# Second picks of the aggregation weighed by VectorE in one instruction a part, and the closing bias laid by two wide products

## The chip, the core and the metric

The kernel runs on one core of one Trainium2 chip. The core has TensorE (PE, matrix products into PSUM), VectorE (DVE), ScalarE (ACT), GpSimd (POOL, here mostly the issuer of indirect and adding DMAs) and SyncE (SP, an issuer of plain DMAs); 16 DMA engines move the data. The metric is the device time of one execution in microseconds, as the median of several runs.

## The reference, cut to what matters

```python
h = relu(layernorm(x))                                   # 6250 nodes x 128
hid  = relu(h[src] @ W1[:128] + h[dst] @ W1[128:] + b1)  # one row per edge, 200000 edges
mask = sigmoid(hid @ W2 + b2)
w    = mask / (segment_sum(mask, src)[src] + 1e-9)
agg  = segment_sum(w[:, None] * h[dst], src)             # <- the aggregation
emb  = where(deg > 0, 0.5 * h + 0.5 * agg, h)
x    = x + relu(emb @ Wl + bl)                           # <- the closing product and its bias
# then layernorm, four graph convolutions by segment_max, and the sum with x
```

## The kernel before, in words

The program has stages one after the other; names of tiles begin with the letter of the stage. Stage a computes the masks of the edges, stage b (from 1720 to 2602 us) aggregates, stage c runs the four convolutions and takes nearly the whole second half. The change lies in stage b alone.

The 6250 nodes are 49 tiles of 128 (TILES = 49), and the targets are seven ranges of seven tiles (RANGES = RANGE = 7; RCOLS = 896 columns). Stage b builds, for each range `cb` and each source tile `u`, a block: a matrix `mass` of 128 source nodes by 896 target nodes that holds mask values. There are 343 blocks, numbered k = 49*cb + u. They go through a ring of 16 buffers (M_RING). One block is made in these steps:

- **heat(k)**, VectorE, L2004: one comparison writes six parts of 128 columns as zeros and ones into `onehot` (three buffers; it waits until ACT has used block k-3, `weighed_made`).
- **ACT, L1924**: six multiplications of one part each, by a mask per partition, into `mass[k % 16]`; it waits first for `hot` and for a free buffer (`wait_free`).
- **weigh_rest(k)**, VectorE, L2013: the seventh part in one instruction, after its own `wait_free`.
- **second picks**: a block whose u is a multiple of seven (TWICE, 49 of the 343) gets a second set. `heat_twice(k)`, VectorE, L2022, compares seven parts into `onehot_2`; ACT weighs them in seven multiplications into `extra` (L1933); `add_extra(k)`, VectorE, L2031, adds `extra` to `mass` in one operation of 896 columns. It stands two blocks later in VectorE's order (EXTRA_LAG = 2), behind `heat(k+2)` and `weigh_rest(k+2)`.
- **POOL, L1894**: when the block is weighed (and, for a block of TWICE, `extra_added`), an adding DMA of 448 KB brings the slow edges' masks from memory on top of the buffer. POOL issues them in the order of k, so a block that is not ready holds all later ones.
- **PE, L1983**: two products of the landed block with `h_row` (512 and 384 columns) add up `agg`; after every fourth block, and after u = 48, `total_bands` (L1956, L1959) adds up the columns into `totals`, and only its last products set `multiplied`, which frees the buffers: the ring is freed in groups of four (`free_by`).

The end of a range is spread over the next one. At u = 8 ACT copies the band sums (`copy_sums`, L1915), for which it must wait until PE has finished all 49 blocks of the range before. At u = 3 PE forms the totals (`total_up`, L1946). At u = 21 VectorE runs `embed` (L2041 to L2052, seven operations, one of them a reciprocal), and during it makes no comparison. PE waits for its result at u = 14 (`multiply`, `emb_made`), since PE stands some blocks behind VectorE. `multiply` forms emb @ Wl + bl: seven products of 128 columns with `wl` (L1968), and behind each a product of one row, ones by `bl` (L1970), that adds the bias. At u = 34 VectorE runs `join` (L2057 and on). For the last range all this follows with nothing beside it, and stage c starts behind it.

In this text block 21 means the block with u = 21 of its range, and 0 is the start of ACT's copy of the band sums in the third range (cb = 2), at 1969.90 us of the trace.

Of the kernel before, what the change touches and what calls it, by code (L numbers as in the profile page):

```python
# [16 lines left out]
P = 128  # L17
NODES = 6250
EDGES = 200000
D = 128  # L20
TILES = -(-NODES // P)
# [27 lines left out]
HEAD, TAIL = 4, 3  # L49
# [79 lines left out]
def bc(ap, shape):  # L129
    return ap.to_broadcast(shape)  # L130


def gnn(nc, x_in, src_in, dst_in, w1_in, b1_in, w2_in, b2_in, wl_in, bl_in,
# [20 lines left out]
    with ExitStack() as whole:  # L154
# [1622 lines left out]
        with ExitStack() as ctx:  # L1777
# [7 lines left out]
            onehot_2 = sb("b_onehot_2", [P, RANGE, P], BF16)  # L1785
            extra = sb("b_extra", [P, RANGE, P])
            ones_first = sb("b_ones_first", [P, P])
# [8 lines left out]
            wl = sb("b_wl", [P, D])  # L1796
            bl = sb("b_bl", [1, D])
            stats = sb("b_stats", [P, RANGE, 6])
# [12 lines left out]
            hot_2 = sem("b_hot_2")  # L1811
            extra_made = sem("b_extra_made")
            extra_added = sem("b_extra_added")
# [28 lines left out]
            def _(sp):  # L1842
                sp.dma_start(wl[:, :], wl_in).then_inc(w_loaded, 16)
                sp.dma_start(bl[:, :], bl_in.rearrange("(o n) -> o n", o=1)).then_inc(w_loaded, 16)

# [58 lines left out]
            def _(act):  # L1904
# [12 lines left out]
                for k in range(BLOCKS):  # L1917
                    cb, u, e = k // TILES, k % TILES, k % 3
                    if cb and u == SUMS_AT:
                        copy_sums(cb - 1)  # L1920
                    act.wait_ge(hot, k + 1)
                    wait_free(act, k)
                    for c in range(SCALED):
                        last = act.mul(mass[k % M_RING][:, c, :], onehot[e][:, c, :],  # L1924
                                       mask_r[:, u, cb * RANGE + c:cb * RANGE + c + 1])
                    last.then_inc(weighed_made, 1)
                    if k in TWICE:
                        i = TWICE.index(k)
                        act.wait_ge(hot_2, i + 1)
                        if i:  # L1930
                            act.wait_ge(extra_added, i)
                        for c in range(RANGE):
                            last = act.mul(extra[:, c, :], onehot_2[:, c, :],  # L1933
                                           mask_2[:, u // RANGE, cb * RANGE + c:cb * RANGE + c + 1])
                        last.then_inc(extra_made, 1)
                    if cb and u == JOIN_AT:
                        finish(cb - 1)
# [4 lines left out]
            def _(pe):  # L1942
# [22 lines left out]
                def multiply(cb):  # L1965
                    pe.wait_ge(emb_made, cb + 1)
                    for c in range(RANGE):
                        pe.matmul(product[cb % 2][:, c, :], emb_t[:, c * P:(c + 1) * P], wl[:, :], start=True,  # L1968
                                  stop=False)
                        last = pe.matmul(product[cb % 2][:, c, :], ones[0:1, :], bl[0:1, :], start=False, stop=True)  # L1970
                    last.then_inc(product_made, 1)
# [24 lines left out]
            def _(dve):  # L1996
# [20 lines left out]
                def heat_twice(k):  # L2017
                    cb, u, i = k // TILES, k % TILES, TWICE.index(k)
                    full, first = [P, RANGE, P], cb * RANGE
                    if i:  # L2020
                        dve.wait_ge(extra_made, i)
                    dve.tensor_tensor(onehot_2[:, :, :],  # L2022
# [3 lines left out]
                def add_extra(k):  # L2026
                    i = TWICE.index(k)
                    dve.wait_ge(weighed_made, k + 1)
                    dve.wait_ge(rest_weighed, k + 1)
                    dve.wait_ge(extra_made, i + 1)  # L2030
                    dve.tensor_tensor(mass[k % M_RING][:, :, :], mass[k % M_RING][:, :, :], extra[:, :, :], ALU.add  # L2031
                                      ).then_inc(extra_added, 1)

# [633 lines left out]
```

## Time and profile before

| what | us |
|---|---|
| median of 3 runs | 4972.48 (4972.26 to 4973.69) |
| the profiled execution | 4971.88 |
| its span in the trace | 4970.1 |
| stage b in it | 1720 to 2602 |
| the copies of the band sums | 1849.8, 1969.9, 2090.6, 2209.7, 2330.7, 2450.0, 2569.2 |

From one copy of the band sums to the next is one period of 49 blocks: 120.1, 120.7, 119.1, 121.0, 119.3 and 119.2 us. In the views below a row of a timeline gives the start in us, the length in us, the engine, the line and what is written from what, with the count of merged instructions and, in brackets, the idle time ahead and what ended it. A table by windows gives for each stretch the busy us of each engine and the number of its instructions, then the granted clock of TensorE (1.00 is 2.4 GHz, 0.50 is 1.2 GHz), the mean busy share of the 16 DMA engines and the GB/s. That share can be a little over one, since packets overlap.

### The profile page before, as it was taken

Reading aid. Unit: us, or ns where it says so; the run is one execution under the profiler, and the core shown is the slowest. Engines: PE = TensorE matmul, PEld = TensorE weight load, DVE = VectorE, ACT = ScalarE, POOL = GpSimd, SP = SyncE. Lnnn points to the kernel's source line nnn. Section 1 sums busy time; section 2 is a strip of 40 time slices with the busy share of each in tenths; the row PEclk is TensorE's granted clock in tenths of the full one; section 3 lists DMA queues with packets and bytes.
Section 4 is the critical chain, followed back from the end, with each engine's and each line's share of the span. In section 5 each row is a group of like instructions: output and inputs, shape, how many; then the busy total and the mean of one; then the engine's idle time right before and its main releaser. Section 6 shows DMA issues by size and latency. Waiting matters only on the chain. (4 is left out here: it accounts for less than half of the span.)

```text
span 4970.1 us, 48372 instructions
## 1 busy us (share of the span) xinstructions
PE 3739.1 (75%) x16011; PEld 1589.9 (32%) x16011; DVE 3885.0 (78%) x5124; ACT 943.7 (19%) x2780; POOL 3103.7 (62%) x3043
## 2 busy tenths in 40 slices
PE   1801068766766399999976989798987898969897
PEld 0401022222222134444432434333433343424343
DVE  4698488877877567777757888798887988878887
ACT  0100010000000198888841000010001000010000
POOL 5200377777777534444435777777776777767777
PEclk9999579988888799999988999899998999989998
DMA  9995365544545399999965444444444444444443
GB/s 361 397 402 233 87 201 168 169 144 145 172 139 154 98 211 206 208 208 209 207 138 157 135 140 136 118 141 132 140 130 126 137 133 133 132 134 135 140 137 95
DMA packets 359755, 843.42 MB, mean 170 GB/s; under 512 B 97017, under 2 KB 174559, under 8 KB 359327
## 3 DMA queue, kind: packets, MB, share of 16 engines
q0 software_dynamic: 137488, 313.46, 29.3%
q1 hardware_dynamic: 172624, 436.91, 24.9%
q10 hardware_dynamic: 49392, 89.94, 5.7%
q8 instruction: 128, 2.10, 0.2%
q14 instruction: 123, 1.01, 0.1%
HBM read 597.79 MB, written 242.28 MB: 169 GB/s over the span
## 5 line engine op out<-in xcount | busy, mean ns | idle before, releaser
L2429 PE MATMUL c_wide<-c_choice,c_parts 128*128 128x512 fp8e4 x8232 | 1881.7, 387 | 283.1 <-DVE c_odd L2514 136.9
L2303 POOL DMA_INDIRECT c_ring<-table,near x1288 | 1293.6, 1004 | 445.7 <-issue 327.9
L2429 PEld LDWEIGHTS c_wide<-c_choice,c_parts 128*128 128x128 bf16 x8232 | 797.8, 99 | 1337.2 <-DVE c_odd L2514 195.8
L2514 DVE TENSOR_TENSOR c_odd<-c_odd,c_wide 128x1024 f32<-128x1024 f32 x644 | 783.5, 1217 | 55.5 <-PE c_wide L2429 52.7
L2514 DVE TENSOR_TENSOR c_even<-c_even,c_wide 128x1024 f32<-128x1024 f32 x672 | 817.5, 1217 | 8.1 <-PE c_wide L2429 1.9
L1529 PE MATMUL a_wide<-a_choice,a_parts 128*128 128x512 fp8e4 x2058 | 526.6, 402 | 181.9 <-DVE a_hidden L1612 168.8
L1924 ACT ACTIVATE b_mass<-b_onehot,mask_r 128x128 f32<-128x128 bf16 x2058 | 607.2, 387 | 100.2 <-DVE b_onehot L2004 73.9
L1983 PE MATMUL b_agg<-b_mass,b_h_row 128*128 128x512 f32 (+1 forms) x1372 | 561.0, 558 | 74.1 <-DMA b_mass<-masks 74.0
L1894 POOL DMA_DIRECT2D b_mass<-masks x343 | 299.6, 962 | 475.5 <-ACT b_mass L1924 359.7
L1612 DVE TENSOR_TENSOR a_hidden<-a_wide,a_minus_bt 128x1024 f32<-128x1024 f32 x343 | 417.1, 1216 | 132.4 <-PE a_wide L1529 132.1
L1414 POOL DMA_INDIRECT masks<-a_value,a_cell x379 | 428.1, 1130 | 115.5 <-issue 114.6
L1406 POOL DMA_INDIRECT a_ring<-table_a,near x322 | 343.0, 1065 | 103.1 <-issue 92.6
L2004 DVE TENSOR_TENSOR b_onehot<-pick_of,up_row 128x768 bf16<-128x768 bf16 x343 | 327.7, 955 | 71.2 <-ACT b_mass L1924 69.3
L1983 PEld LDWEIGHTS b_agg<-b_mass,b_h_row 128*128 128x128 f32 x1372 | 254.0, 193 | 375.8 <-issue 290.7
L2368 ACT ACTIVATE c_h_t<-c_product,c_b 128x512 f32<-128x512 f32 (+1 forms) x56 | 35.5, 634 | 1775.3 <-PE c_product L2459 1775.3
L2543 DVE TENSOR_TENSOR c_ring<-c_ring 128x256 f32<-128x256 f32 (+5 forms) x444 | 219.2, 494 | 194.5 <-DMA c_ring<-table,near 167.9
L1529 PEld LDWEIGHTS a_wide<-a_choice,a_parts 128*128 128x128 bf16 x2058 | 192.7, 101 | 540.0 <-issue 359.9
L2303 POOL DMA_INDIRECT c_ring<-table,near_left x228 | 231.8, 1017 | 78.8 <-issue 64.4
L1602 DVE TENSOR_SCALAR a_choice<-a_pick_row,one_up 128x1024 fp8e4<-128x1024 bf16 x343 | 271.0, 791 | 0.0
L1548 PE MATMUL a_logits<-a_hidden,a_w_col 128*32 128x512 f32 x1372 | 205.5, 696 | 69.8 <-DVE a_hidden L1612 69.7
L786 POOL DMA_INDIRECT meta<-record,rank x49 | 47.1, 961 | 330.8 <-DVE rank L856 316.2
L2314 POOL DMA_INDIRECT table<-c_new,row_info x147 | 150.9, 1027 | 57.2 <-issue 43.3
(352 smaller groups left out, 2992.5 us busy)
## 6 DMA issues: line engine op xcount, KB each, us to landing
c_choice<-chosen SPq DMA_DIRECT2D x196, 896.0 KB
masks<-n_zeros SPq DMA_DIRECT2D x196, 784.0 KB, 8.0
b_mass<-masks POOLq DMA_DIRECT2D x343, 448.0 KB, 11.6
a_pick_row<-picks ACTq DMA_DIRECT2D x343, 256.0 KB
chosen<-a_choice SPq DMA_DIRECT2D x49, 896.0 KB, 5.4
c_ring<-table,near POOLq DMA_INDIRECT x1288
c_source<-table SPq DMA_DIRECT2D x28, 448.0 KB, 6.0
c_own_rows<-own_xh SPq DMA_DIRECT2D x14, 448.0 KB, 6.0
```

What stands on the lines that cost most here:

```text
L1406: pool.indirect_dma_start(ring[:, at + j, :], None, table_a, bass.IndirectOffsetOnAxis(list_of(u)[:, j:j + 1], 0)).then_inc(landed[u % A_F ...
L1414: pool.indirect_dma_start(mask_cells, bass.IndirectOffsetOnAxis(cell[:, u, j:j + 1], 0), value[:, at:at + 1], None).then_inc(cells_stored, 16)
L1529: last = pe.matmul(wide[q][:, lo_c:hi_c], parts[:, s, part, :], choice[e][:, s % CHUNK, lo_c:hi_c], start=(part == 0), stop=(part == 2))
L1602: dve.tensor_scalar(choice[m % 3][:, s, :], pick_row[n % A_PICKS][:, :], one_up[:, :], None, ALU.is_equal, saturate=False).then_inc(choice ...
L1612: dve.tensor_tensor(hidden[:, n % A_HIDDEN, :], wide[n % 2][:, 0:WCOLS], minus_bt[:, a, :], ALU.max).then_inc(taken, 1)
L1894: pool.dma_start(flat[e], masks[u * P:(u + 1) * P, cb * RCOLS:(cb + 1) * RCOLS], accum_op=ALU.add).then_inc(mass_loaded[e], 16)
L1924: last = act.mul(mass[k % M_RING][:, c, :], onehot[e][:, c, :], mask_r[:, u, cb * RANGE + c:cb * RANGE + c + 1])
L1983: pe.matmul(agg[cb % 2][:, lo_c:hi_c], h_row[:, u, :], flat[e][:, lo_c:hi_c], start=(u == 0), stop=(u == TILES - 1))
L2004: dve.tensor_tensor(onehot[e][:, :, :], bc(pick_of[:, u, first:first + SCALED].unsqueeze(2), full), bc(up_row[:, :].unsqueeze(1), full), A ...
L2303: pool.indirect_dma_start(ring[:, at + j, :], None, table1[layer % 2], bass.IndirectOffsetOnAxis(of_u[:, j:j + 1], 0)).then_inc(landed[n % ...
L2429: last = pe.matmul(wide[q][:, lo_c:hi_c], parts[:, s, part, :], choice[e][:, s % CHUNK, lo_c:hi_c], start=(part == 0), stop=(part == 2))
L2514: dve.tensor_tensor(side[:, :], side[:, :], found, ALU.max).then_inc(taken, 1)
```

## The change

ACT no longer weighs the second picks, and `extra` and its semaphore are gone. `add_extra`, at the same place in VectorE's order, now runs seven instructions instead of one: each multiplies a part of `onehot_2` by its mask and adds it to the part of `mass`. `heat_twice` waits for the last `add_extra` in place of ACT. In `multiply` the bias comes first, as two products of one row over 512 and 384 columns with `start=True`, and the seven products with `wl` add to them; `bl` is loaded seven times side by side.

```diff
-            extra = sb("b_extra", [P, RANGE, P])
-            bl = sb("b_bl", [1, D])
+            bl = sb("b_bl", [1, RANGE, D])
+            bl_row = bl[:, :, :].rearrange("p c m -> p (c m)")
...
-                sp.dma_start(bl[:, :], bl_in.rearrange("(o n) -> o n", o=1)).then_inc(w_loaded, 16)
+                sp.dma_start(bl[:, :, :], bc(bl_in.rearrange("(p o n) -> p o n", p=1, o=1), [1, RANGE, D])
+                             ).then_inc(w_loaded, 16)
...
-                    if k in TWICE:
-                        i = TWICE.index(k)
-                        act.wait_ge(hot_2, i + 1)
-                        if i:
-                            act.wait_ge(extra_added, i)
-                        for c in range(RANGE):
-                            last = act.mul(extra[:, c, :], onehot_2[:, c, :],
-                                           mask_2[:, u // RANGE, cb * RANGE + c:cb * RANGE + c + 1])
-                        last.then_inc(extra_made, 1)
...
                     pe.wait_ge(emb_made, cb + 1)
+                    for lo_c, hi_c in ((0, BANK), (BANK, RCOLS)):
+                        pe.matmul(agg[cb % 2][:, lo_c:hi_c], ones[0:1, :], bl_row[0:1, lo_c:hi_c], start=True, stop=False)
                     for c in range(RANGE):
-                        pe.matmul(product[cb % 2][:, c, :], emb_t[:, c * P:(c + 1) * P], wl[:, :], start=True,
-                                  stop=False)
-                        last = pe.matmul(product[cb % 2][:, c, :], ones[0:1, :], bl[0:1, :], start=False, stop=True)
+                        last = pe.matmul(product[cb % 2][:, c, :], emb_t[:, c * P:(c + 1) * P], wl[:, :], start=False,
+                                         stop=(c in (HEAD - 1, RANGE - 1)))
...
                     if i:
-                        dve.wait_ge(extra_made, i)
+                        dve.wait_ge(extra_added, i)
...
                 def add_extra(k):
-                    i = TWICE.index(k)
+                    cb, u, i = k // TILES, k % TILES, TWICE.index(k)
                     dve.wait_ge(weighed_made, k + 1)
                     dve.wait_ge(rest_weighed, k + 1)
-                    dve.wait_ge(extra_made, i + 1)
-                    dve.tensor_tensor(mass[k % M_RING][:, :, :], mass[k % M_RING][:, :, :], extra[:, :, :], ALU.add
-                                      ).then_inc(extra_added, 1)
+                    dve.wait_ge(hot_2, i + 1)
+                    for c in range(RANGE):
+                        s = cb * RANGE + c
+                        last = dve.scalar_tensor_tensor(mass[k % M_RING][:, c, :], onehot_2[:, c, :],
+                                                        mask_2[:, u // RANGE, s:s + 1], mass[k % M_RING][:, c, :],
+                                                        ALU.mult, ALU.add)
+                    last.then_inc(extra_added, 1)
```

ACT's order, before, in the third range from block 7 to block 15 (`b_mass9` is block 7's buffer):

```order
L1924 ACTIVATE b_mass9<-b_onehot0,mask_r 128x128 x6
L1933 ACTIVATE b_extra<-b_onehot_2,mask_2 128x128 x7
L1915 COPY b_band_sums<-b_totals1 128x896
L1924 ACTIVATE b_mass10<-b_onehot1,mask_r 128x128 x6
L1924 ACTIVATE b_mass11<-b_onehot2,mask_r 128x128 x6
L1924 ACTIVATE b_mass12<-b_onehot0,mask_r 128x128 x6
L1924 ACTIVATE b_mass13<-b_onehot1,mask_r 128x128 x6
L1924 ACTIVATE b_mass14<-b_onehot2,mask_r 128x128 x6
L1924 ACTIVATE b_mass15<-b_onehot0,mask_r 128x128 x6
L1924 ACTIVATE b_mass0<-b_onehot1,mask_r 128x128 x6
L1933 ACTIVATE b_extra<-b_onehot_2,mask_2 128x128 x7
L1924 ACTIVATE b_mass1<-b_onehot2,mask_r 128x128 x6
```

The same place now:

```order
L1924 ACTIVATE b_mass9<-b_onehot0,mask_r 128x128 x6
L1915 COPY b_band_sums<-b_totals1 128x896
L1924 ACTIVATE b_mass10<-b_onehot1,mask_r 128x128 x6
L1924 ACTIVATE b_mass11<-b_onehot2,mask_r 128x128 x6
L1924 ACTIVATE b_mass12<-b_onehot0,mask_r 128x128 x6
L1924 ACTIVATE b_mass13<-b_onehot1,mask_r 128x128 x6
L1924 ACTIVATE b_mass14<-b_onehot2,mask_r 128x128 x6
L1924 ACTIVATE b_mass15<-b_onehot0,mask_r 128x128 x6
L1924 ACTIVATE b_mass0<-b_onehot1,mask_r 128x128 x6
L1924 ACTIVATE b_mass1<-b_onehot2,mask_r 128x128 x6
```

The groups of seven behind blocks 7 and 14 are gone; nothing else on ACT moved.

VectorE's order behind `embed` of the third range, before (`b_mass7` is block 21's buffer):

```order
L2052 TENSOR_TENSOR b_emb_t<-b_emb_t,b_h_t1 128x896
L2004 TENSOR_TENSOR b_onehot0<-pick_of,up_row 128x768
L2013 TENSOR_SCALAR b_mass8<-up_row,b_pick_f,mask_r 128x128
L2004 TENSOR_TENSOR b_onehot1<-pick_of,up_row 128x768
L2013 TENSOR_SCALAR b_mass9<-up_row,b_pick_f,mask_r 128x128
L2031 TENSOR_TENSOR b_mass7<-b_mass7,b_extra 128x896
L2004 TENSOR_TENSOR b_onehot2<-pick_of,up_row 128x768
```

The same place now:

```order
L2048 TENSOR_TENSOR b_emb_t<-b_emb_t,b_h_t1 128x896
L1996 TENSOR_TENSOR b_onehot0<-pick_of,up_row 128x768
L2005 TENSOR_SCALAR b_mass8<-up_row,b_pick_f,mask_r 128x128
L1996 TENSOR_TENSOR b_onehot1<-pick_of,up_row 128x768
L2005 TENSOR_SCALAR b_mass9<-up_row,b_pick_f,mask_r 128x128
L2025 SCALAR_TENSOR_TENSOR b_mass7<-b_onehot_2,mask_2,b_mass7 128x128 x7
L1996 TENSOR_TENSOR b_onehot2<-pick_of,up_row 128x768
```

The place is the same; one operation of 896 columns became seven of 128.

PE's order at `multiply` now, between block 14 and block 15 (before, seven pairs of L1968 and L1970 of 128 columns stood here):

```order
L1975 MATMUL b_agg0<-b_mass0,b_h_row 128x384
L1959 MATMUL b_agg1<-b_bl,ones 128x512
L1959 MATMUL b_agg1<-b_bl,ones 128x384
L1961 MATMUL b_agg1<-b_wl,b_emb_t 128x128 x7
L1975 MATMUL b_agg0<-b_mass1,b_h_row 128x512
```

Fourteen products became nine, with the wait for `emb_made` ahead of them as before.

## Rows read from the trace of the kernel before

**Rows 1.** Table by windows: a stretch of the first range, and the third period.

```profile
1795.00:1805.00 10.00, 9.29 (x36) 3.63 (x35) 6.57 (x11) 10.00 (x36) 3.85 (x5) 1.00 1.08 212
...
1969.90:2090.60 120.70, 114.51 (x425) 50.27 (x426) 91.29 (x140) 102.42 (x347) 52.84 (x57) 0.93 1.04 208
```

**Rows 2.** Table by windows of 3 us in the third period.

```profile
2007.00:2010.00 3.00, 3.00 (x10) 2.10 (x10) 3.00 (x6) 2.42 (x9) 0.00 (x0) 0.50 1.02 198
2010.00:2013.00 3.00, 3.00 (x10) 2.10 (x9) 3.00 (x6) 3.00 (x12) 2.52 (x3) 0.50 0.44 62
2013.00:2016.00 3.00, 3.00 (x10) 2.01 (x9) 2.71 (x6) 3.00 (x11) 1.85 (x3) 0.50 1.03 183
2016.00:2019.00 3.00, 3.00 (x6) 1.61 (x6) 0.68 (x1) 2.19 (x8) 1.37 (x2) 0.50 1.00 194
...
2028.00:2031.00 3.00, 3.00 (x20) 0.91 (x20) 2.34 (x5) 3.00 (x12) 1.73 (x2) 1.00 0.42 64
```

**Rows 3.** Waits in 1720 to 2610 us: total us, times, longest us.

```profile
DVE b_mass L2031 <- ACT b_extra L1933: 91.4, 43, 2.7
...
ACT b_mass L1924 <- DVE b_onehot L2004: 73.9, 7, 25.0
...
PE b_agg L1968 <- DVE b_emb_t L2052: 43.7, 7, 12.5
...
ACT b_mass L1924 <- PE b_totals L1959: 26.3, 6, 5.2
...
DVE b_xh L2057 <- PE b_agg L1970: 10.3, 1, 10.3
```

**Rows 4.** Timeline of ACT in the third period.

```profile
1969.90 0.91 ACT L1915 COPY b_band_sums<-b_totals 128x896 f32<-128x896 f32 x1 [0.67 <-PE b_totals L1959]
1970.71 12.37 ACT L1924 ACTIVATE b_mass<-b_onehot,mask_r 128x128 f32<-128x128 bf16 x42
1982.98 2.14 ACT L1933 ACTIVATE b_extra<-b_onehot,mask 128x128 f32<-128x128 bf16 x7
1985.02 12.37 ACT L1924 ACTIVATE b_mass<-b_onehot,mask_r 128x128 f32<-128x128 bf16 x42
...
2023.06 1.86 ACT L1924 ACTIVATE b_mass<-b_onehot,mask_r 128x128 f32<-128x128 bf16 x6 [4.87 <-PE b_totals L1959]
```

**Rows 5.** Timeline of VectorE around embed, and the rows that price the series.

```profile
1992.16 0.96 DVE L2004 TENSOR_TENSOR b_onehot<-pick_of,up_row 128x768 bf16<-128x768 bf16 x1 [0.53 <-ACT b_mass L1924]
...
2007.71 0.95 DVE L2004 TENSOR_TENSOR b_onehot<-pick_of,up_row 128x768 bf16<-128x768 bf16 x1
...
2008.84 1.09 DVE L2031 TENSOR_TENSOR b_mass<-b_mass,b_extra 128x896 f32<-128x896 f32 x1
2009.84 0.95 DVE L2004 TENSOR_TENSOR b_onehot<-pick_of,up_row 128x768 bf16<-128x768 bf16 x1
...
2034.61 1.45 DVE L2062 BATCH_NORM_STATS2 b_stats<-b_xh 128x6 f32<-128x128 f32 x7
```

**Rows 6.** Groups by line, VectorE: 128 columns with two masks.

```profile
L2013 DVE TENSOR_SCALAR b_mass<-up_row,b_pick_f,mask_r 128x128 f32<-128x128 bf16 x343 | 119.2, 348 | 41.4 <-PE b_totals L1959 41.4
```

**Rows 7.** Timeline of PE in the third period.

```profile
2006.73 0.79 PE L1968 MATMUL b_agg<-b_wl,b_emb_t 128*128 128x128 f32 x2 [5.19 <-DVE b_emb_t L2052]
...
2016.85 3.35 PE L1983 MATMUL b_agg<-b_mass,b_h_row 128*128 128x512 f32 x4
...
2020.14 2.70 PE L1959 MATMUL b_totals<-b_mass,ones 128*32 128x512 f32 x16
```

**Rows 8.** Timeline of POOL in the third period.

```profile
2010.48 3.61 POOL L1894 DMA_DIRECT2D b_mass<-masks  x4 [13.69 <-DVE b_mass L2031]
...
2018.49 0.85 POOL L1894 DMA_DIRECT2D b_mass<-masks  x1 [0.90 <-ACT b_mass L1924]
2028.80 1.73 POOL L1894 DMA_DIRECT2D b_mass<-masks  x2 [9.46 <-ACT b_mass L1924]
```

**Rows 9.** One line's instructions: duration in ns, min/median/max.

```profile
L1894 POOL DMA_DIRECT2D b_mass<-masks x343: 853/862/1962, 1729.4 to 2554.3; - x172
```

More of the change, by code:

```diff
@@ L1811, in gnn @@
             hot_2 = sem("b_hot_2")
-            extra_made = sem("b_extra_made")
             extra_added = sem("b_extra_added")
```

## The prediction

> **What bounds the kernel now.** I read the tables by windows first, then the waits, then the timelines of one period. The table by windows shows who is full in stage b. In the first range the DMA engines show a busy share of 1.08 at 212 GB/s, and elsewhere where nothing holds them 1.07 to 1.08; I take 1.075 as full. There ACT is busy without a pause too, 10.00 of 10, and PE 9.29 [rows 1]. Over a whole later period of 120.7 us the DMA share is 1.04, PE is busy 114.5 us and ACT 102.4 us [rows 1]. So three engines are near full, and the question is which one waits for the others. A full DMA would need 120.7 x 1.04 / 1.075 = 116.8 us for what it moves in this period; some 4 us of it are lost. The small windows show where: from 2007 to 2019 the share is 1.02, 0.44, 1.03 and 1.00, a loss of (0.055 + 0.635 + 0.045 + 0.075) x 3 / 1.075 = 2.3 us (**gap A**), and in 2028 to 2031 it is 0.42, a loss of 1.8 us (**gap B**) [rows 2]. The sum, 4.1 us, agrees with the whole period.
>
> The timelines say why. POOL issues nothing for 13.7 us until 2010.48, held by the sum of block 21, which stands behind `embed` on VectorE; and again nothing for 9.5 us until 2028.80, held by block 28 [rows 8]. Block 28 found no free buffer until 2023.06, after ACT had waited 4.87 us for PE [rows 4], because PE had waited 5.19 us for `embed` and then ran `multiply` from 2006.73 to 2016.85 [rows 7], 10.12 us, at a granted clock of 0.50 [rows 2], which is the 1.2 GHz level. These waits come back in each of six periods: PE's total of 43.7 us less the 12.5 of the end is 5.2 each, ACT's wait for the comparison is (73.9 - 25.0) / 6 = 8.2 each, and its wait for a buffer is 26.3 / 6 = 4.4 [rows 3]. So the period is the DMA's work plus the two gaps. The engine whose work is reduced, ACT, is not the bound by itself; what counts is when it lets `embed` start.
>
> **The change part by part.** All times below are in the third period, from the copy at 1969.90 [rows 4].
>
> ACT loses the groups of seven. One takes 1985.02 - 1982.98 = 2.04 us; the blocks themselves take 12.27 us for seven, 1.75 each [rows 4]. Per period that is 7 x 2.04 = 14.3 us, but nearly all of it turns into idle time: at u = 8 ACT waits for PE's end of the range before (0.67 us here), and whatever ACT has gained by then it waits longer there. What is left is the group of block 14, the only one between the copy and the comparison of block 21. That comparison starts at 1992.16 when ACT has done block 18 [rows 5]; now 2.04 us earlier. `embed` has a fixed length, so it ends 2.04 us earlier too.
>
> VectorE gets seven instructions for one, 49 times. Bounds: seven statistics of 128 columns each take 1.45 us in a row [rows 5]; seven of the length of the 128-column operation with two masks, end to end, would take 7 x 0.348 = 2.4 us [rows 6]. A seven-fold run hides the tail of each in the next, so I am near the lower row and take 1.7 us, against 1.00 us that the sum took from one start to the next (2008.84 to 2009.84) [rows 5]. Where nobody waits for VectorE this costs nothing: it now waits 91.4 us in all for ACT's extra parts [rows 3], which is more than 49 x 0.7 = 34 us. If that cover were gone it would cost these 34 us. The comparisons of block 14 to 16 fall together with a series, but VectorE stands 0.53 us idle at each comparison [rows 5] and is three comparisons ahead, so the start of `embed` keeps its 2.04 us.
>
> Gap A: the issue of block 21 waits for the end of its series. Before: 2010.48. Now 2.04 earlier by `embed`, 0.7 later by the series: 1.3 us earlier. The DMA's queue runs empty at the same moment as before, since blocks up to 20 were issued in time, so gap A shrinks from 2.3 to 1.0 us. Bounds: 2.04 + (1.00 - 1.45) = 1.6 us gained, or 2.04 - 1.4 = 0.6 us.
>
> `multiply`: at the half clock one product of 128 columns is 10.12 / 14 = 0.72 us. The seven of `wl` stay, 5.1 us. The two wide ones do the columns of one block's pair, 2020.14 - 2016.85 = 3.3 us at the same clock [rows 7], so 8.4 us for 10.1, a gain of 1.7 us. If PE's shorter wait (5.19 - 2.04 = 3.15 us) keeps the clock at 1.00, it is about half, 4.2 us; no row here shows a wait of that length, so I count the half clock and keep the other as the better end.
>
> Gap B: PE finishes `multiply` 2.04 + 1.7 = 3.7 us earlier, so the buffer for block 28 comes at 2019.3 instead of 2023.06. Before, ACT then took 1.75 + 2.04 us and VectorE's sum 1 us. Now VectorE works off the comparisons and last parts of blocks 29 and 30, 1.13 us each (2008.84 - 2007.71 [rows 5]), and the series of 1.7 us: the issue comes at about 2024.1, 4.7 us earlier than 2028.80. The queue would run empty 1.3 us earlier than before, since gap A is shorter. Issue and emptiness thus move by 4.7 and 1.3 us, and a gap of 1.8 us is filled (3.4 us against 1.8). Gap B goes, with 1.6 us to spare.
>
> What is late next: PE. Its own line in a period is at most 120.7 - 3.7 = 117.0 us. The DMA's is 120.7 - 1.3 - 1.8 = 117.6. PE is 0.6 us short of being the bound, so the DMA's line holds. A higher clock on PE would not bring more than the rest of gap A.
>
> One period thus loses 3.1 us, and there are six: 18.6 us. The end of the last range has nothing beside it: `join` waits the whole 10.3 us of `multiply` [rows 3], and gains 1.7 us. The first range is bound by the full DMA [rows 1] and its loads, and gains nothing I can count (at most the 2 us by which block 0 is earlier). The sevenfold load of `bl` is 3.5 KB at the start of the stage, beside others: nothing. Sum: 18.6 + 1.7 = 20.3 us. The profiled execution took 4971.88 us, 0.6 below the median of 4972.48: 4971.9 - 20.3 = 4951.6, which against the median is **4952 us**, 0.41% less.
>
> One rule speaks against the change. POOL's 343 issues take 853 ns at least, 862 in the median and 1962 at most [rows 9], while VectorE runs comparisons with two inputs beside them all the time; most are not lengthened. The Trainium skill (SBUF — State Buffer, section "SBUF: two separate sides") says that VectorE and GpSimd share a pair of SBUF ports under an exclusive lock, which a VectorE operation with two SBUF inputs holds against a GpSimd operation that reads SBUF, and that descriptors of GpSimd's DMAs can be starved by it. By the row nothing changes; by the rule the added operations would hold POOL as well, which is the third rival below, at 4958 instead of 4952 us.
>
> **The rivals.**
> - **Both gaps go.** If the series costs 1.45 us and PE keeps its clock, what is left of A also shrinks, and the longest measure of loss, 4.1 us a period, goes whole: 6 x 4.1 + 1.7 + 2 for the start = 28 us, 4944 us. For it: the two gaps are the only stretches below 1.0. Against: `embed` still stops the comparisons for 12 us.
> - **The series is dear or `embed` does not move.** At 2.4 us the series takes 0.7 us a period off gap A, and if VectorE is late at blocks 14 to 16, `embed` moves by 1 us instead of 2: A shrinks by nothing, B by 1 to 1.8 us. 6 x 1.4 + 1.7 = 10 us, 4962 us. For it: gap A hangs on VectorE alone.
> - **POOL held by VectorE's ports.** If an issue right behind a series waits for the next comparison, 0.95 us [rows 5], gap A shrinks by 0.35 us, and B goes as forecast: 6 x (0.35 + 1.8) + 1.7 = 15 us, 4958 us. Against: the median of 862 ns [rows 9].
> - **No change.** The DMA loses the same elsewhere: freed from the gaps it meets PE, which is 0.6 us from being the bound, and PE stays longer at the half clock. Then only the end gains, 1.7 us: 4971 us. For it: PE is busy 114.5 of 120.7 us.
> - **Slower.** On VectorE `add_extra(k)` stands behind `weigh_rest(k+2)`, which waits for a free buffer, and POOL holds all blocks behind k. ACT and VectorE now reach the full ring sooner, so blocks 14 and 42, whose k+2 opens a group of four, are held. It costs from the point at which POOL's queue is shorter than the hold; at 4.4 us (two blocks) for two places in seven ranges it is 61 us, less the 20 gained: 5013 us. Against: at those places some eight blocks are issued and not yet summed.
>
> **How the numbers follow.** Forecast 0.50 (own range 4947 to 4957), both gaps 0.14, dear series 0.12, ports 0.06, no change 0.13, slower 0.05. The range reaches from just under the better end, 4941, to the upper side of the dear series, 4965, which leaves out the no-change and slower cases. What can be told from no change is about 0.2%, 10 us, that is below 4962.5: the forecast, both gaps, ports and half of the dear series, 0.76; within it the other half and no change, 0.19; slower 0.05.
>
> **What would show it.** In the changed profile: comparison 21 some 20.2 us behind the copy of the band sums instead of 22.3; PE's wait for `embed` 3.1 us instead of 5.2; `multiply` 8.4 us at clock 0.50 or about 4.2 at 1.00; seven operations of 0.2 to 0.3 us in the series; POOL's first issue after `embed` at 39.3 us instead of 40.6; a DMA window of low share there that is shorter, and none at block 28; ACT idle at the copy for over 10 us; periods of about 117.5 us. Wrong would be periods as before with the gaps gone (then the DMA's rate fell or PE binds), a series over 2.4 us, or a new stretch of low DMA share at blocks 14 or 42.

## The result, and the profile after

| | before | changed |
|---|---|---|
| median (lowest to highest) of 8 runs, us | 4972.58 (4959.39 to 4982.92) | 4952.85 (4941.64 to 4960.23) |
| ratio to before, 95% interval | | 0.996 (0.9946 to 0.9975) |
| profiled execution's span | 4970.1 | 4955.1 |
| first comparison of stage b | 1722.7 | 1731.2 |
| stage b, from it to ACT's last relu | 879.2 | 855.6 |
| its six periods together | 719.5 | 698.9 |
| from the last copy of the band sums to ACT's last relu | 32.7 | 29.2 |

The change gains 0.4%, about 20 us, and the whole 95% interval of the ratio lies below 1. The single runs of one kernel differ by up to 24 us. In the profiled executions the stages ahead of stage b, whose code is the same, end between 1722.7 and 1737.5 us, and the time behind stage b varies between 2363 and 2376 us. So the span of one execution can't settle a few microseconds, but stage b can, and below kernels are compared by it. In it the change gains 23.6 us: 20.6 in the six periods, 3.6 at the end, less 0.4 in the stretch up to the first copy, which is longer, and rounding.

The table by windows of the changed kernel, by periods (columns as in [rows 1]):

```profile
1858.70:1975.20 116.50, 110.26 (x415) 46.95 (x415) 94.51 (x179) 89.91 (x298) 51.52 (x56) 0.96 1.07 215
1975.20:2091.30 116.10, 108.12 (x416) 45.67 (x415) 94.56 (x179) 88.41 (x297) 51.26 (x56) 0.99 1.06 213
2091.30:2208.40 117.10, 108.12 (x415) 45.59 (x415) 94.69 (x179) 88.39 (x297) 51.76 (x56) 0.99 1.07 214
...
sum 698.90, PE 654.28 PEld 277.26 DVE 549.80 ACT 517.78 POOL 300.92; mean PE 109.05 PEld 46.21 DVE 91.63 ACT 86.30 POOL 50.15
```

The third period, the second row, answers to [rows 1]: the DMA share rose from 1.04 to 1.06, PE is busy 108.1 us instead of 114.5 and ACT 88.4 instead of 102.4. The windows of 3 us around `embed` answer to [rows 2]:

```profile
2011.00:2014.00 3.00, 3.00 (x15) 2.45 (x14) 3.00 (x11) 3.00 (x11) 0.00 (x0) 0.70 1.06 207
2014.00:2017.00 3.00, 3.00 (x12) 1.50 (x14) 3.00 (x6) 2.52 (x9) 2.38 (x3) 0.74 0.54 81
2017.00:2020.00 3.00, 3.00 (x21) 1.23 (x14) 2.95 (x6) 3.00 (x12) 2.03 (x3) 1.00 1.04 188
...
2032.00:2035.00 3.00, 3.00 (x21) 0.95 (x20) 2.28 (x14) 2.47 (x10) 1.19 (x3) 1.00 1.07 201
```

One gap is left, (0.015 + 0.535 + 0.035) x 3 / 1.075 = 1.6 us in this period. Gap B, which stood at 58 us behind the copy of the band sums, is gone: at 57 us (the last row) the share is 1.07. Over the first five periods, a period less what its DMA share would need at 1.075, the idle DMA fell from 4.7 us a period to 1.3. The third period is not quite the mean: over all six, the idle DMA from 36 to 48 us behind the copy (gap A) fell from 2.9 us to 1.2, and from 54 to 66 us (gap B) from 1.8 to under 0.1.

The timeline of the third period, against [rows 4, 5, 7, 8]; its copy of the band sums is at 1975.25:

```profile
1975.25 0.91 ACT L1915 COPY b_band_sums<-b_totals 128x896 f32<-128x896 f32 x1 [11.56 <-PE b_totals L1950]
...
1995.47 0.96 DVE L1996 TENSOR_TENSOR b_onehot<-pick_of,up_row 128x768 bf16<-128x768 bf16 x1 [0.54 <-ACT b_mass L1924]
...
2010.04 1.77 PE L1959 MATMUL b_agg<-b_bl,ones 1*128 1x512 f32 x4 [3.17 <-DVE b_emb_t L2048]
2011.74 2.99 PE L1961 MATMUL b_agg<-b_wl,b_emb_t 128*128 128x128 f32 x14
2012.15 1.92 DVE L2025 SCALAR_TENSOR_TENSOR b_mass<-b_onehot,mask,b_mass 128x128 f32<-128x128 bf16 x7
2013.99 0.95 DVE L1996 TENSOR_TENSOR b_onehot<-pick_of,up_row 128x768 bf16<-128x768 bf16 x1
2014.62 3.55 POOL L1894 DMA_DIRECT2D b_mass<-masks  x4 [14.53 <-ACT b_mass L1924]
```

In these rows one fp32 product of 128 columns counts as two records, so x14 is seven products. The comparison of block 21 stands 20.22 us behind the copy (22.3 before), PE waits 3.17 us for `embed` (5.19), the series takes 1.84 us from start to start, and POOL goes on 39.37 us behind the copy (40.6). The row names ACT as what released POOL, which is the semaphore event that came last by the profile; but ACT had weighed block 21 before its wait that ends at 2010.9, and in order POOL waits for block 21's series, which ends at 2014.07 (2012.15 + 1.92), 0.55 us ahead of the issue, as the sum did before (2009.93 and 2010.48). ACT's gain went into its wait at the copy, 11.56 us instead of 0.67. The waits of the whole stage, against [rows 3]:

```profile
ACT b_band_sums L1915 <- PE b_totals L1950: 95.7, 7, 28.2
...
PE b_agg L1959 <- DVE b_emb_t L2048: 31.4, 7, 12.5
...
ACT b_mass L1924 <- PE b_totals L1950: 25.6, 15, 3.5
...
DVE b_xh L2053 <- PE b_agg L1961: 6.7, 1, 6.7
```

The last row is the end: VectorE's `join` waits 6.7 us for `multiply` instead of 10.3.

### The profile page after: what moved, and what is told of

Read it like the earlier page. It is cut to its first block and busy times, and to the rows that moved or that the text cites. A ratio compares the mean times of both kernels' runs of the same rounds, so it can differ in the third digit from the quotient of the medians.

```text
span 4955.1 us, 48135 instructions
## 1 busy us (share of the span) xinstructions
PE 3719.1 (75%) x15941; PEld 1566.0 (32%) x15941; DVE 3918.8 (79%) x5418; ACT 847.3 (17%) x2437; POOL 3108.0 (63%) x3043
## 5 line engine op out<-in xcount | busy, mean ns | idle before, releaser
L1529 PE MATMUL a_wide<-a_choice,a_parts 128*128 128x512 fp8e4 x2058 | 539.6, 410 | 176.6 <-DVE a_hidden L1612 163.4
L1406 POOL DMA_INDIRECT a_ring<-table_a,near x322 | 360.8, 1120 | 103.6 <-issue 86.9
```

Of the source, the lines that this page charges most:

```text
L1406: pool.indirect_dma_start(ring[:, at + j, :], None, table_a, bass.IndirectOffsetOnAxis(list_of(u)[:, j:j + 1], 0)).then_inc(landed[u % A_F ...
L1529: last = pe.matmul(wide[q][:, lo_c:hi_c], parts[:, s, part, :], choice[e][:, s % CHUNK, lo_c:hi_c], start=(part == 0), stop=(part == 2))
```

## The experiments

**Theory 1**: a period lasts as long as the DMA's work and the time for which the DMA runs dry; it ran dry twice, behind `embed` (gap A), where POOL's issue hangs on VectorE, and at block 28 (gap B), where it hangs on how early PE is done with `multiply`. **Rivals**: PE's work or its clock sets the period; one half of the change does it all; VectorE's added work is on the path at every block of second picks. All numbers of stage b come from one profiled execution each. "Each" is PE's wait for `embed` in one period, and the end runs from the last copy to ACT's last relu.

| kernel | six periods, us | PE's wait, each | end, us | stage b, us | median of runs, us |
|---|---|---|---|---|---|
| before | 719.5 | 5.2 | 32.7 | 879.2 | 4972.58 (8) |
| changed | 698.9 | 3.2 | 29.2 | 855.6 | 4952.85 (8) |
| picks only | 701.6 | 3.2 | 32.7 | 861.3 | 4960.45 (8) |
| bias only | 706.5 | 5.2 | 29.2 | 863.8 | 4958.50 (10) |
| bias grouped | 706.3 | 5.2 | 29.2 | 862.6 | 4953.20 (1) |
| shifted pairs | 714.7 | 5.2 | 32.1 | 873.9 | 4969.85 (1) |
| multiply at 17 | 698.9 | 0 | 29.1 | 855.5 | 4956.40 (1) |
| embed at 17 | 697.1 | 0 | 29.2 | 853.9 | 4957.84 (5) |
| series twice | 716.0 | 4.4 | 29.2 | 872.3 | 4972.83 (1) |
| less DMA | 661.1 | 3.2 | 29.2 | 805.2 | 4902.33 (1) |
| embed at 17, early pairs grouped | 697.2 | 0 | 29.2 | 853.9 | 4950.26 (5) |

### Each half alone

```diff
 (picks only: the changed kernel with multiply and the load of bl as before)
-                    for lo_c, hi_c in ((0, BANK), (BANK, RCOLS)):
-                        pe.matmul(agg[cb % 2][:, lo_c:hi_c], ones[0:1, :], bl_row[0:1, lo_c:hi_c], start=True, stop=False)
```

> The change without its second half: VectorE weighs the second picks, the bias stays seven products of one row behind the seven of wl. Theory 1 (the period is the DMA's work plus what it idles; the picks let embed start 2 us earlier, and that fills the second gap): periods of 116 to 117 us as in the changed kernel, PE waits 3.2 us for embed, the end keeps its 10.2 us of multiply; stage b from the first comparison to ACT's last relu 859 us (879.3 before, 855.6 changed), so about 20 us under the kernel before. Rival (the shorter multiply is what frees the buffers in time): periods of 118.5 us or more, stage b 870 us or more.

```diff
 (bias only: the kernel before with the changed multiply and load of bl)
+                    for lo_c, hi_c in ((0, BANK), (BANK, RCOLS)):
+                        pe.matmul(agg[cb % 2][:, lo_c:hi_c], ones[0:1, :], bl_row[0:1, lo_c:hi_c], start=True, stop=False)
```

> The other half alone: ACT weighs the second picks as before, the bias is two wide products ahead of the seven. Theory 1: embed does not move, PE still waits 5.2 us for it and its clock falls, gap A (about 2.3 us of idle DMA behind embed) stays, but multiply is some 3.5 us shorter, which fills most of gap B; periods of 118 to 119 us, the end 3.6 us shorter, stage b about 865 us. Rival (the picks do it all): periods of 120 us as before and only the end shorter, stage b 875.7 us.

Both are faster than before, by ratios of 0.9969 (0.9958 to 0.9979) and 0.997 (0.9961 to 0.998). Sum rows of their six periods:

```profile
sum 701.60, PE 680.74 PEld 300.30 DVE 549.72 ACT 519.07 POOL 300.22; mean PE 113.46 PEld 50.05 DVE 91.62 ACT 86.51 POOL 50.04
```

```profile
sum 706.50, PE 656.28 PEld 280.38 DVE 521.09 ACT 596.82 POOL 304.65; mean PE 109.38 PEld 46.73 DVE 86.85 ACT 99.47 POOL 50.78
```

The first row is picks only: 17.9 us less than before, with PE as busy as before (680.7 against 683.4 us). The second is bias only: 13.0 us less, with ACT as busy as before. Together they bring 20.6, not 30.9: each takes most or all of gap B, which can be filled only once. With the bias alone the small windows show gap A as before (0.44 in the third period) and 1.01 where gap B was; with the picks alone 0.74 and 0.99. Both rivals of these runs fall. The end follows the bias alone: 32.7 with the pairs, 29.2 without.

These two runs leave open what bounded the kernel before, and the waits of PE answer a part of it. PE's rows over the six periods, of the kernel before, of picks only, of bias only and of the changed kernel:

```profile
PE b_agg L1968 <- DVE b_emb_t L2052: 31.2, 6, 5.3
PE b_agg L1983 <- DMA b_mass<-masks: 4.7, 8, 0.7
...
PE b_agg L1957 <- DVE b_emb_t L2045: 19.0, 6, 3.2
PE b_agg L1972 <- DMA b_mass<-masks: 1.8, 4, 0.7
...
PE b_agg L1986 <- DMA b_mass<-masks: 18.9, 25, 1.3
...
PE b_agg L1975 <- DMA b_mass<-masks: 25.5, 31, 1.3
```

Before, PE's work (683.4), its wait for `embed` (31.2) and its wait for the DMA (4.7) add up to 719.3 of the 719.5 us: PE had work or waited for `embed` in all but 0.8 us of a period. With the picks alone the same sum is 680.7 + 19.0 + 1.8 = 701.5 of 701.6. So in these two kernels PE was as much the limit as the DMA, and a faster DMA alone could have taken off no more than those 4.7 and 1.8 us. The gain of picks only can as well be read as PE's: 12.2 us of its wait, 2.7 of its work and 2.9 of its wait for the DMA. Only with the shorter `multiply` does PE wait for the DMA by 3 to 4 us a period, so only there does the DMA's line stand clearly above PE's. No run takes DMA work off the kernel before, so there the two limits are not separated.

### Is PE's wait, or its clock, on the path?

```diff
-        TOTAL_AT, MULTIPLY_AT = 3, 14
+        TOTAL_AT, MULTIPLY_AT = 3, 17
```

> The changed kernel with PE's multiply at u = 17 instead of 14, so that PE has no wait for embed while embed itself stays where it is. Theory 1 (the DMA's work and the gap behind embed set the period; PE's wait and its clock do not): the clock stays at 1.00 through the stage, PE's wait goes from 3.2 to 0, and the periods stay at 116 to 117 us, their sum within 3 us of 698.9. Rival (PE's wait and the fall of its clock are on the path): periods shorter by 3 us or more.

```profile
1977.80:2093.80 116.00, 107.93 (x415) 43.58 (x415) 94.55 (x179) 88.32 (x297) 51.35 (x56) 1.00 1.06 213
...
sum 698.90, PE 647.65 PEld 262.00 DVE 549.01 ACT 517.56 POOL 300.81; mean PE 107.94 PEld 43.67 DVE 91.50 ACT 86.26 POOL 50.14
```

PE no longer waits, the granted clock is 1.00 in every period instead of 0.96 to 0.99, and the six periods take 698.9 us, as in the changed kernel. The time went into PE's wait for the DMA, which rose from 25.5 to 51.0 us over the six periods. In the changed kernel neither PE's wait nor its clock costs time.

### Is it the DMA?

```diff
-                    pool.dma_start(flat[e], masks[u * P:(u + 1) * P, cb * RCOLS:(cb + 1) * RCOLS],
+                    pool.dma_start(flat[e][:, 0:BANK], masks[u * P:(u + 1) * P, cb * RCOLS:cb * RCOLS + BANK],
```

> The changed kernel with an adding DMA that brings only 512 of the 896 columns of each block (the masks of the other 384 columns are left out of the sum); all engines do the same work. Theory 1 (the DMA's work sets the period, PE is next): the DMA share falls under 0.8 and the periods fall to PE's own line, 49 x 1.96 + 1.8 + 1.1 + multiply 4.5 + wait 3.2 = 107 us. Rival (PE already sets the period): periods of 115 us or more.

```profile
1954.60:2066.60 112.00, 108.78 (x415) 47.41 (x416) 94.76 (x179) 88.50 (x298) 51.26 (x56) 0.95 0.78 136
...
2286.40:2395.60 109.20, 105.97 (x415) 46.42 (x415) 94.70 (x179) 88.29 (x297) 51.35 (x56) 0.98 0.80 140
```

This kernel leaves out the slow edges' masks of 384 of the 896 columns. With the same instructions on all engines and 57% of the bytes of each adding DMA, the periods fall to between 110.6 and 112.0 us in the first three and 109.2 in the last three, and the first range, up to its copy, from 127.5 to 114.9 us. There PE is the bound: 106.0 busy and 3.2 of wait for `embed` make 109.2, and 108.8 and 3.2 make 112.0; it never waits for the DMA. The forecast of this run, 107, was 2 to 5 us low, but the rival (115 or more) falls. So in the changed kernel the DMA's work sets the period, and PE's own line stands some 4 to 7 us below it.

### What is left behind `embed`

```diff
-        EMBED_AT, JOIN_AT = 21, 34
+        EMBED_AT, JOIN_AT = 17, 34
```

> The changed kernel with VectorE's embed at u = 17 instead of 21, so that it is done before PE needs it, and block 21 no longer waits behind it. Theory 1: PE does not wait for embed, the clock stays at 1.00, the last gap in the DMA's work (1.6 us a period) goes, periods of 114.5 to 115.5 us, stage b about 847 us, 8 us less than changed, 4945 us. Rival (what is left of a period is not that gap but PE's work or the DMA's own rate at other places): periods stay at 116 to 117 us.

```profile
sum 697.10, PE 647.64 PEld 262.13 DVE 548.99 ACT 516.87 POOL 299.80; mean PE 107.94 PEld 43.69 DVE 91.50 ACT 86.15 POOL 49.97
```

PE's wait is gone and the clock is 1.00, as expected, but only 1.8 us are gained in the six periods, not 8. My expectation took the one period that I had looked at (1.6 us) for all; the mean was 1.3, and 0.7 of it stays. In the third period it is a window of 0.72 at 30 us behind the copy, where `embed` now stands. The DMA's own work, a period less its idle time, is 115.2 us there and 115.5 here. The shares have two digits, and 0.01 of a period is 1.1 us, so a few tenths can't be split further. Its median of 4957.84 us can't be told from the changed kernel's.

```diff
                     for c in range(RANGE):
                         s = cb * RANGE + c
+                        dve.scalar_tensor_tensor(spare[:, c, :], onehot_2[:, c, :],
+                                                 mask_2[:, u // RANGE, s:s + 1], mass[k % M_RING][:, c, :],
+                                                 ALU.mult, ALU.add)
+                    for c in range(RANGE):
+                        s = cb * RANGE + c
```

> The changed kernel with a second series of seven VectorE instructions ahead of each series, written to a buffer that nobody reads: 1.84 us more at each block of second picks. Theory 1 (VectorE's work is covered everywhere but behind embed, where POOL's issue of block 21 hangs on it): VectorE's 7 x 1.84 = 12.9 us more a period show as 1.5 to 2 us, the DMA's gap behind embed grows from 1.3 to about 3.1 us, the sum of the six periods is 708 to 712 us against 698.9. Rival (VectorE's work is on the path at every block of second picks): the periods grow by 5 us or more. Rival 2 (the gap behind embed costs nothing): they stay within 0.5 us.

```profile
2011.37 0.95 DVE L1997 TENSOR_TENSOR b_onehot<-pick_of,up_row 128x768 bf16<-128x768 bf16 x1
...
2013.62 1.92 DVE L2026 SCALAR_TENSOR_TENSOR b_spare<-b_onehot,mask,b_mass 128x128 f32<-128x128 bf16 x7
2015.46 1.92 DVE L2031 SCALAR_TENSOR_TENSOR b_mass<-b_onehot,mask,b_mass 128x128 f32<-128x128 bf16 x7
2017.30 0.95 DVE L1997 TENSOR_TENSOR b_onehot<-pick_of,up_row 128x768 bf16<-128x768 bf16 x1
```

The periods take 716.0 us, 17.1 more, or 2.9 each: more than the 1.5 to 2.2 of theory 1 and much less than the 12.9 us of added work. The missing part shows in PE's wait for `embed`, which rose from 3.2 to 4.4 us: the comparison of block 21 now comes 21.5 us behind the copy and not 20.2. With the doubled series of block 21 itself that makes 1.84 + 1.3 = 3.1 us, and gap A grew from 1.2 to 4.5 us, by 3.3. The doubled series of block 14 is the only added work between the copy and that comparison, so VectorE's cover at blocks 14 to 16 holds for one series of 1.84 us and not for two. The place of the cost is as the theory has it, behind `embed`; the cover ahead of it was thinner than I thought. Doubled, the series eats 16.7 of the 23.6 us that the change gains in stage b (872.3 us, between 855.6 and 879.2).

### Why multiply became so short

The wide products take what was forecast, 3.3 us at the half clock, but the seven with `wl` take 0.48 us each there and not 0.72. The end of the changed kernel:

```profile
2572.83 3.35 PE L1959 MATMUL b_agg<-b_bl,ones 1*128 1x512 f32 x4 [12.47 <-DVE b_emb_t L2048]
...
2576.11 3.36 PE L1961 MATMUL b_agg<-b_wl,b_emb_t 128*128 128x128 f32 x14
...
2579.50 1.09 DVE L2053 SCALAR_TENSOR_TENSOR b_xh<-b_agg,b_xh 128x896 f32<-128x896 f32 x1 [6.73 <-PE b_agg L1961]
```

Either the narrow bias products are dear, or changing from one kind to the other is.

```diff
 (bias grouped: the kernel before)
                     for c in range(RANGE):
-                        pe.matmul(product[cb % 2][:, c, :], emb_t[:, c * P:(c + 1) * P], wl[:, :], start=True,
+                        pe.matmul(product[cb % 2][:, c, :], emb_t[:, c * P:(c + 1) * P], wl[:, :], start=(c in (0, HEAD)),
                                   stop=False)
-                        last = pe.matmul(product[cb % 2][:, c, :], ones[0:1, :], bl[0:1, :], start=False, stop=True)
+                    for c in range(RANGE):
+                        last = pe.matmul(product[cb % 2][:, c, :], ones[0:1, :], bl[0:1, :], start=False,
+                                         stop=(c in (HEAD - 1, RANGE - 1)))
```

> The kernel before with its fourteen products of multiply in another order: the seven of wl in a row, then the seven of one row with the bias (the zeroing start flag only at the first part of each bank). Theory 1 (changing between a full product and one of a single row costs 0.24 us each at the half clock; 0.72 us a product in pairs against 0.48 in a row): multiply in the end takes 14 x 0.48 = 6.8 us instead of 10.2. Rival (a narrow product costs 0.72 us wherever the rest is in memory, and the wide ones alone bring the gain): 10.2 us, or about 8.4 if only the products of one row are dear.

```profile
2573.66 3.35 PE L1968 MATMUL b_agg<-b_wl,b_emb_t 128*128 128x128 f32 x14 [12.47 <-DVE b_emb_t L2054]
2576.94 3.35 PE L1971 MATMUL b_agg<-b_bl,ones 1*128 1x128 f32 x14
```

All fourteen narrow products, in two groups, take 6.6 us: the same as the two wide and seven narrow ones, and 706.3 us of periods against 706.5. The wide form brings nothing of its own; taking the kinds apart brings it all. The next kernel has the same start flags and alternates again, but never adds to the addresses just written.

```diff
 (shifted pairs: the kernel before)
+                    for c in range(RANGE + 1):
+                        if c < RANGE:
+                            pe.matmul(product[cb % 2][:, c, :], emb_t[:, c * P:(c + 1) * P], wl[:, :],
+                                      start=(c in (0, HEAD)), stop=False)
+                        if c:
+                            last = pe.matmul(product[cb % 2][:, c - 1, :], ones[0:1, :], bl[0:1, :], start=False,
+                                             stop=(c in (HEAD, RANGE)))
```

> The kernel before with multiply's products still alternating between a full one and one of a single row, but each bias product for the part before, so that no product adds to the addresses that the one just ahead of it wrote. If the 0.24 us a product come from the change between 128 rows and one row (the weights of another height), multiply in the end stays at 10.2 us. If they come from adding at once to the same addresses in PSUM, it falls to about 6.7 us as with the grouped order.

```profile
2585.25 1.22 PE L1969 MATMUL b_agg<-b_wl,b_emb_t 128*128 128x128 f32 x4 [12.47 <-DVE b_emb_t L2055]
2586.40 0.79 PE L1972 MATMUL b_agg<-b_bl,ones 1*128 1x128 f32 x2
2587.12 0.80 PE L1969 MATMUL b_agg<-b_wl,b_emb_t 128*128 128x128 f32 x2
2587.85 0.79 PE L1972 MATMUL b_agg<-b_bl,ones 1*128 1x128 f32 x2
...
2593.64 1.22 PE L1972 MATMUL b_agg<-b_bl,ones 1*128 1x128 f32 x4
```

The alternating products still start 0.72 us apart, and only the two of one kind at either end share one change less. So it is the change between the two kinds, 0.24 us each at the half clock, and neither the address nor the start flags. The kinds are a product over 128 rows and one over a single row; they differ in their operands too, and no run changes the rows alone, so that the rows are the reason is argued and not shown. The periods agree: 714.7 us, near the 719.5 of before, and PE's work fell by as much (683.4 to 678.4 us).

### A version with two more edits

```diff
-        EMBED_AT, JOIN_AT = 21, 34
+        EMBED_AT, JOIN_AT = 17, 34
...
                         for c in range(n):
                             pe.matmul(product[q][:, c, :], h_t[:, (t + c) * P:(t + c + 1) * P], w1[:, :],
-                                      start=True, stop=False)
-                            last = pe.matmul(product[q][:, c, :], ones[0:1, :], b1[0:1, :], start=False,
-                                             stop=True)
+                                      start=(c % 2 == 0), stop=False)
+                        for c in range(n):
+                            last = pe.matmul(product[q][:, c, :], ones[0:1, :], b1[0:1, :], start=False,
+                                             stop=(c % 2 == 1 or c == n - 1))
```

> The changed kernel with two more edits: embed at u = 17, and the same kind of product pairs in an early stage (L551 and L553, 49 products of 256 columns and 49 of one row, from 120 to 260 us) grouped instead of alternating. For the first: stage b as with embed at 17, 854 us. For the second: the products get shorter, the first group of eight from 8.8 to about 6.9 us, but ACT waits 92.6 us there for DMA stores (the fourth pass and on), so only the first three passes can show it: 0 to 8 us earlier, and nothing where those stores are the bound. In all 2 to 10 us under the changed kernel, 4943 to 4951 us; rival: no difference to be told from the changed kernel's 4953.

Two rows of ACT's timeline in the early stage, of the changed kernel and of this one:

```profile
129.19 0.59 ACT L524 COPY record<-f_product 128x512 f32<-128x512 f32 x1 [8.82 <-PE f_product L553]
...
173.69 0.59 ACT L524 COPY record<-f_product 128x512 f32<-128x512 f32 x1 [17.54 <-DMA table_a<-f_node_a]
```

```profile
126.09 0.59 ACT L524 COPY record<-f_product 128x512 f32<-128x512 f32 x1 [5.13 <-PE f_product L554]
...
173.56 0.59 ACT L524 COPY record<-f_product 128x512 f32<-128x512 f32 x1 [32.78 <-DMA table_a<-f_node_a]
```

ACT's first wait for the products fell from 8.8 to 5.1 us, more than the 6.9 forecast, and the wait for the store, which ends at 173.6 us in both, took it all. The median of 4950.26 us, ratio 0.9953 (0.994 to 0.9967) to before, is the lowest here, but its interval overlaps the changed kernel's (0.9946 to 0.9975). It can't be called faster than the change, so the rival stands.

## Why the prediction was right

The forecast was 4952 us, the median is 4952.85. By its steps, each against the third period or the end:

- **The bound**: right for the changed kernel. There the DMA's work and its gaps set the period, shown by less DMA (661.1 us) and by the run with `multiply` at 17 (no change with PE's wait and clock fall gone). For the kernel before it is half of the account: "the period is the DMA's work plus the two gaps" is an account that holds whatever the limit is, and PE, busy or waiting for `embed` for 119.1 of 119.9 us, was as near a limit. The forecast price holds either way, since the DMA's line is where the period ends up.
- **ACT**: right. Its gain went into the wait at the copy, and the one group of block 14 moved the comparison of block 21 by 2.0 us.
- **VectorE's series**: 1.84 us, forecast 1.7. Each instruction starts 0.26 us after the last. The series needs 49 x 0.8 = 41 us more of VectorE, and the DMA runs dry for it nowhere but behind `embed`.
- **Gap A**: POOL's issue at 39.37 us, forecast 39.3. In the third period the gap is 1.6 us, forecast 1.0: it shrank by 0.7 us while the issue moved by 1.2, so there the queue ran dry some 0.5 us earlier too. The premise that it runs empty at the same moment as before doesn't hold from one period to the next: the issue comes within 0.02 us at the same place in all six, while the gap is 2.2 to 4.1 us long before and 0.6 to 1.8 after. The means, 2.9 and 1.2, give 1.7 us gained, forecast 1.3; why the moment varies is open.
- **multiply**: the term that was mis-sized. Forecast 8.4 us at the half clock, measured 6.6 at the end. I gave the seven products of `wl` the 0.72 us of the alternating pairs; they take 0.48. In the periods it takes 4.7 to 6.6 us, since the clock falls late or briefly: PE starts it at full speed after its 3.2 us wait in the third period (1.70 us for the wide pair).
- **Gap B**: gone, as forecast, but with more to spare. The issue of block 28 came 51.2 us behind the copy instead of 58.9, 7.7 us earlier; forecast was 4.7. The terms that the prediction lists (the buffer at 2019.3, twice 1.13 and the series of 1.7) give 2023.3 and not its 2024.1; the measured place is 2021.1 on that scale. In all six periods it is 51.1 to 51.2, whether `multiply` takes 4.7 or 6.6 us, so PE no longer holds it; with the picks alone it is 55.0 to 56.4.
- **What is late next**: PE was put at 117.0 us a period at most, 0.6 from the bound. In the changed kernel its work and its wait for `embed` are 109.0 + 3.2 = 112.2 us and it waits 4.3 for the DMA; with less DMA it stands at 109.2. The rival "no change" hung on this margin, and it was some 4 to 7 us wide. That it was is owed to `multiply`, mis-sized by 1.9 us: with the picks alone PE stands at 113.46 + 3.17 = 116.6 of 116.9 us, as near the bound as was feared.
- **The sum**: 18.6 + 1.7 = 20.3 us forecast (1.3 and 1.8 us a period for the gaps, measured 1.7 and 1.7), 20.6 + 3.6 measured, less 0.4 to the first copy, in stage b. The median moved by 19.7. That it lies so close is partly luck: medians of eight runs that spread over 19 to 24 us are no measure of a microsecond.
- **Ports**: POOL's 343 issues take 865 ns in the median and 853 at least, against 862 and 853 in [rows 9]; the longest is 2634 ns. The issue behind the series started 0.63 us after the next comparison (2014.62 and 2013.99), while that was still running, and not behind it. The five issues that ran beside a series took 905 to 929 ns, the five beside the sum before 918 to 934. The longest ones stand in bunches of overlapping issues, and some of over 2 us ran while VectorE did nothing. The rule that the prediction quotes from the Trainium skill (SBUF — State Buffer, "SBUF: two separate sides") lets a VectorE operation with two SBUF inputs hold only a GpSimd operation that reads SBUF; no issue here shows such a hold.

```profile
L1894 POOL DMA_DIRECT2D b_mass<-masks x343: 853/865/2634, 1738.1 to 2535.1; - x172
```

- **Slower by held blocks**: in the first five periods no window with a DMA share under 1.0 stands anywhere but at 39 to 45 us, behind `embed`, so none at blocks 14 or 42.

## What to carry to other kernels

When several engines look full, find the stretches where the fullest resource runs dry, and price an edit by how much earlier the work reaches it there; two edits that fill the same gap don't add up. Add up the next engine's work and waits as well: where they fill the period, as PE's did before, it is a second limit, and its margin decides what filling the gaps is worth. Taking 14.3 us of work a period off ACT was worth what one group of 2.04 us ahead of `embed` moved. Here, in fp32 at the half clock, products of one row, such as a bias, were better kept in a group than between full ones, wide or not; and a shorter product behind a store that is late anyway gives nothing.

## What the runs showed of the hardware

- In fp32, with 128 columns at 1.2 GHz, products of one kind start 0.47 us apart, and products that alternate between 128 rows and one row 0.72 us, whether or not they write the same addresses. In the kernel before PE stayed at 0.50 through all 10.2 us of `multiply`; with the same 5.2 us of wait ahead of it and the kinds apart, `multiply` took 5.2 to 6.6 us and the mean clock of the periods rose from 0.93 to 0.96.
- After a wait of 3.2 us PE ran on at full speed at first in some periods (the wide pair in 1.70 us) and at the half clock in others (3.3 us), within one execution. After 5.2 us it was slow at first in 17 of 18 periods (before, bias only, bias grouped); in the third period of bias grouped's six the first product was already partly fast.
- VectorE's multiply-and-add of 128 fp32 columns, with a mask per partition, takes 0.346 us and starts 0.26 us after the one ahead (median of 343, changed kernel).
